# Identity products on TensorE ahead of five local stages, elements 0 and 1, in a two-layer sequence kernel

## What is computed

```python
xn = layernorm(x)
x = x + gated_linear_attention(xn) + local_transformer(xn)     # layer 0
xn = layernorm(x)
x = x + delta_rule_attention(xn) + switch_head_attention(xn)   # layer 1
```

```python
q, k, v = split(shift_token(x) @ wqkv)
q, k = rotary(l2norm(q) * qs), rotary(l2norm(k) * ks)
x = x + softmax(q @ k.T in the window) @ v @ wo
a, g = split(layernorm(shift_token(x)) @ w1 + b1)
x = x + (a * gelu(g)) @ w2 + b2
```

## Time and profile before

| | us |
|---|---|
| median of 3 runs | 1227.69 (1219.04 to 1230.57) |
| the profiled execution | 1230.62 |
| its span, first to last instruction | 1229.3 |
| mean granted TensorE clock in it | 0.98 of full speed |

### The profile page before, as it was taken

How to read it: one execution, slowest core, us unless ns; L and a number is a source line. 1 busy time by engine, 2 the same in 40 slices (tenths; PEclk the granted TensorE clock), 3 DMA queues, 4 the chain that set the end, 5 groups by cost and what they waited for, 6 DMA issues and landing times.

```text
span 1229.3 us, 30949 instructions
## 1 busy us (share of the span) xinstructions
PE 1153.7 (94%) x11842; PEld 918.7 (75%) x11842; DVE 906.9 (74%) x1894; ACT 704.4 (57%) x2020; POOL 837.9 (68%) x1156
## 2 busy tenths in 40 slices
PE   5887879999989999999999999999999999999998
PEld 3454558887768878777887887887778977788886
DVE  4947888986788868975587688987678766764544
ACT  5787787566756564466654666456776433332222
POOL 3745378688688745699579728699659837874870
PEclk9888889999999999999999999999999999999999
DMA  7101085765546575864478447785346867886763
GB/s 263 35 24 50 6 268 181 215 193 173 168 139 194 201 224 172 259 215 152 137 235 258 147 164 254 221 264 171 124 120 225 263 193 249 249 283 211 263 235 106
DMA packets 91186, 230.67 MB, mean 188 GB/s; under 512 B 9888, under 2 KB 16160, under 8 KB 90912
## 3 DMA queue, kind: packets, MB, share of 16 engines
q1 hardware_dynamic: 90896, 228.11, 57.8%
q10 hardware_dynamic: 144, 0.59, 0.1%
HBM read 225.51 MB, written 3.15 MB: 186 GB/s over the span
## 4 chain that ended last, share of the span: by engine, by line
PE 28%; DVE 12%; DMA 5%; POOL 4%; ACT 4%; issue 3%; SPq 1%; DVEq 0%; POOLq 0%; ACTq 0%
PE bank L896 8%; PE bank L943 6%; DVE ogate L1351 2%; PE bank L824 2%; POOL vgate L1737 2%; DMA kv<-values 2%; PE bank L933 2%; PE bank L914 2%; DMA vgate<-gates 2%; PE bank L610 1%; PE bank L924 1%; DVE kv L1120 1%; PE bank L907 1%; PE bank L669 1%; DMA gates<-xn 1%
## 5 line engine op out<-in xcount | busy, mean ns | idle before, releaser
L1737 POOL TENSOR_TENSOR vgate<-vgate,xT 128x512 f32<-128x512 f32 x256 | 324.9, 1293 | 68.7 <-DMA vgate<-gates 68.6
L896 PE MATMUL bank<-wv,vgate 128*128 128x128 f32 x2048 | 253.0, 278 | 0.6 <-POOL vgate L1737 0.4
L896 PEld LDWEIGHTS bank<-wv,vgate 128*128 128x128 f32 x2048 | 244.4, 193 | 9.6 <-issue 4.5
L943 PE MATMUL bank<-ogate,wo 128*128 128x256 f32 x1024 | 243.1, 383 | 1.7 <-DVE ogate L1351 1.4
L943 PEld LDWEIGHTS bank<-ogate,wo 128*128 128x128 f32 x1024 | 188.3, 190 | 31.8 <-issue 6.8
L1351 DVE TENSOR_TENSOR ogate<-ogate,bank 128x1024 f32<-128x1024 f32 x128 | 152.2, 1213 | 25.7 <-PE bank L933 19.1
L1621 ACT ACTIVATE mprob<-bank,mmin 128x256 f32<-128x256 f32 x128 | 59.3, 469 | 122.2 <-DVE mmin L1340 122.1
L1462 ACT ACTIVATE prob<-prob,mx 128x128 f32<-128x128 f32 (+1 forms) x256 | 96.0, 377 | 37.8 <-DVE mx L1056 37.4
L1669 POOL TENSOR_TENSOR rot<-rot 128x512 f32<-128x512 f32 x64 | 81.5, 1273 | 44.6 <-DVE rot L1032 44.5
L610 PE MATMUL bank<-wqkv,hT 128*128 128x512 f32 x192 | 107.0, 664 | 2.5 <-ACT hT L1398 1.4
L1714 POOL TENSOR_TENSOR dlt<-dlt,step 128x126 f32<-128x126 f32 (+22 forms) x248 | 92.8, 374 | 19.4
(11 more groups left out here) (224 smaller groups left out, 2354.2 us busy)
## 6 DMA issues: line engine op xcount, KB each, us to landing
ogate<-gates SPq DMA_DIRECT2D x128, 512.0 KB, 4.5
vgate<-gates SPq DMA_DIRECT2D x128, 512.0 KB, 4.4
wo<-in_wo_moe SPq DMA_DIRECT2D x128, 256.0 KB, 4.9
wv<-in_wv_moe SPq DMA_DIRECT2D x128, 256.0 KB, 4.8
kv<-values SPq DMA_DIRECT2D x64, 256.0 KB, 5.4
local<-in_local SPq DMA_DIRECT2D x1, 1715.0 KB, 9.5
wqkv<-in_wqkv SPq DMA_DIRECT2D x2, 768.0 KB, 6.4
x<-in_x SPq DMA_DIRECT2D x8, 128.0 KB, 5.0
```

What stands on the lines that cost most here:

```text
L896: i = nc.tensor.matmul(out[:, n * D:(n + 1) * D], xg[:, e, n * P:(n + 1) * P], m.wv[slot][:, e, :], start=(q, n, e) == (0, 0, 0), stop=(q, ...
L943: i = nc.tensor.matmul(out[:, 0:T], m.wo[slot][:, e, :], cg[:, e, :], start=(h, q, e) == (0, 0, 0), stop=(h, q, e) == (MH - 1, 1, EQ - 1))
L1737: i = tt(gate[:, e:e + half, :], gate[:, e:e + half, :], spread(m.xT[b % 2][:, :], 1, half), ALU.mult)
```

## The change

A helper `fill` issues one 128x128 product of the identity with itself into the first 128 columns of the bank that the stage has just taken. Five stages call it between the wait for the bank and the wait for the data, for elements 0 and 1 alone. The stage's own products then overwrite the result. No semaphore, bank or turn changes.

```diff
+    def fill(b, out):
+
+        if b < 2:
+            nc.tensor.matmul(out[:, 0:P], ident, ident, start=True, stop=True)
...
     def qkT(b, l, n, k):
         bank = banks.of("qkT", b, l, n, k)
         out = take(bank)
+        fill(b, out)
         pe.wait_ge(s.rot_scaled, nth("scale", b, l, n, k))
...
     def probT(b, l, w):
         out, p = take(bank), prob_of(m, b, l, w)
+        fill(b, out)
         pe.wait_ge(s.snorm, nth("score", b, l, w))
...
     def pv(b, l, w):
         out = take(bank)
+        fill(b, out)
         pe.wait_ge(t.emptied, t.use)
...
     def lnorm(b, l):
         out = take(bank)
+        fill(b, out)
         pe.wait_ge(s.h2shift, nth("hff", b, l))
...
     def hnT(b, l):
         take(bank)
+        fill(b, bank.ap)
         pe.wait_ge(h.emptied, h.use)
```

## The result

The changed kernel takes 1232.4 us, the median of 20 runs, against 1225.6 us for the kernel before, also the median of 20. The ratio is 1.0058, with a 95% interval of [1.0042, 1.0074]: 7.1 us slower by the ratio, 6.8 us by the two medians. That is within 1% and within the predicted range. But the forecast was "no change", and the interval excludes it. One execution of the changed kernel, 1653.9 us at a mean granted clock of 0.65, was in a slow state and is left out of the ratio; the other 19 lie between 1226.0 and 1240.8 us.

What follows compares the result with a forecast made beforehand. TensorE was taken to set the pace from about 176 us, after a chain passing between engines. 1230.6 + 3.0 - 3.2 = 1230.4 us against the profiled execution, 2.9 us above the median, gave 1227.5 us, no change; range 1216 to 1238.

Steps and rivals of the forecast that it cites:

- +3.0 - 3.2 = -0.2 us: Early part: uncovered fills in four unbroken TensorE runs cost 3.0 us; two clock falls gone or halved give back 3.2 us.
- the falls at 99.1 and 170.8 us: Early half-clock pieces: the one at 170.8 us gone, 1.6 us; the one at 99.1 us half gone, 1.6 us.
- The piece from 31 us: Half-clock piece after waits at 28 to 32 us: two fills, issued by 29.4 us, leave most of 3.29 us empty.
- 17 fills cost nothing: Early waits for data: 17 of 56 fills fall into 17 waits, nearly all longer than 0.24 us, which hide them.
- Removed: nothing. Moved: nothing, on any engine or queue: Whole kernel: the change only adds 56 fills, 13.7 us of TensorE work, and removes or moves nothing.
- Loss: Early part: 39 uncovered fills delay the stages, 10.8 us, to 1238.5 us, or 1241.8 us with another clock fall; chance 0.10.
- No effect on the clock: Early waits: two or three products are too little, the clock falls where it fell; 1230.7 us, chance 0.18.
- Gain: Early part: fills keep the clock up almost everywhere; 1218.7 us, or 1210.5 us if every cold us counts; chance 0.22.
- The last sentence of the prediction: If line 896's first product comes on time yet the end moves over 5 us, the dense part changed for an unnamed reason.

Runs made afterwards that it cites:

- the 17 alone: The changed kernel with products only at the 17 stages that had a wait ahead of them, the other 39 left out: 1230.4 us, ratio 1.0035 to before.
- elements 4 and 5: The change's 56 products issued for elements 4 and 5, whose local stages lie in the dense part, instead of 0 and 1: 1243.6 us, ratio 1.0133 to before.

## Why the prediction was wrong

**Cost and clock came out as a small balance.** The forecast was +3.0 - 3.2 = -0.2 us. The clean measurement is the change with 72 empty waits, +0.7 us give or take 2.5. That shows the balance, not its two terms: both may be small, or larger and equal. The mean granted clock did rise, to 0.985 in the 19 runs of the change and 0.987 in the 12 with the 72 waits, from 0.982 in the 88 runs of before on three chips and 0.980 with 184 empty waits. As forecast, the falls at 99.1 and 170.8 us went; one more, near 119 us, was not expected to. These pieces prove little by themselves, since the profile with 184 empty waits and no product lacks the last two as well. What is left at half clock before 180 us sums to some 31 us instead of 44.2. The piece from 31 us stayed although two fills stand ahead of it, as argued. The line "17 fills cost nothing" fits too: at 1.0035 the 17 alone lose as much as 61 instructions that do no work, at 1.0036, with the gap in the same burst.

**The step that failed** is the opening of the sum: "Removed: nothing. Moved: nothing, on any engine or queue", and with it "what it can delay is that stage and all of TensorE's work behind it until the next wait absorbs the delay". It counts instructions by their duration alone. They also have a place in a stream that is fetched in packets of 256, and 184 more of them move every border behind. The term left out measures 5.6 us, between 2.7 and 8.6, with 184 empty waits and no product. With the 0.7 us of the products and no shift it makes 6.3 us, for 7.1 measured, which the intervals do not tell apart. The profile carried the warning in a row that the prediction never used, q8 with its 95 packets.

**The rivals.** "Loss" foresaw a loss, by uncovered products that move the waits; it would have left the change with the 72 waits as slow as the change, and that one is level with before. Its 10.8 us were never approached, except in elements 4 and 5, where few waits are left and 17.1 us were lost. "No effect on the clock" is refuted by the mean clocks of the runs just given. "Gain" described a change that was not made: with the waits really full the clock up to 180 us is 0.97 to 0.99, and the gain is 3 to 5 us and not the 9 or 17 us of that case. The rule of the Trainium skill's "TensorE: Matmul & The Clock Gate", Terms, would give about 22 us for the same 44.2 us, an estimate from that rule; with nearly all of them warm the runs gained 3 to 5 us and decide against it here. That the rest lies where other engines set the pace is the likely reason and wasn't isolated.

**The last sentence of the prediction** did its work: the product came on time, the end moved by over 5 us in the medians, and that pointed into the dense part.

**Open.** What sets the 5 to 6.5 us. In the change no packet came through q8 between 1075.8 and 1093.5 us. That pause alone is not lateness, since TensorE took 17.6 us for the 256 instructions up to 1090.0 us; then it took 2.0 us for the next 256. The queue of the data was near full in that time:

```profile
q1 hardware_dynamic: 1828, 4.78, 84.3%
q14 instruction: 1, 0.01, 0.2%
```

and in the next 5.4 us two came at once:

```profile
q1 hardware_dynamic: 599, 1.56, 77.9%
q8 instruction: 2, 0.03, 2.4%
```

That the data transfers hold a packet up is likely but not shown. The kernel with the 94 products has two stretches in which TensorE took 256 instructions in about 4 us, the first without a gap at its end and the second with one of 1.1 us:

```profile
422.00:425.80 3.80, 3.80 (x138) 3.59 (x134) 1.38 (x4) 2.54 (x8) 0.00 (x0) 1.00 0.12 39
1092.10:1096.50 4.40, 4.40 (x145) 4.09 (x134) 2.31 (x6) 1.17 (x3) 4.32 (x4) 1.00 1.02 378
```

The DMA engines are busy for 0.12 of the first and all of the second. But at 4.1 us and a share of 0.98 the first profile of before has no gap either, and no run took the transfers away.

The link from the gap in single profiles to the medians is argued, from the sizes (about 4 us of gap for 5.6 us) and from the places, which follow the length of the stream. The single profiles don't bear it out by their times: the one with 184 empty waits has the gap and is the fastest of its twelve runs (1224.1 us), the one of the change with 72 waits has none and is the slowest of its twelve (1231.0 us). From the first product of line 896 or its like to the end, before takes 1053.0 us without the gap and the change 1050.1 us with it. What scatters the executions of one kernel by 5 us around their median is open too.

## What to carry to other kernels

Adding instructions to a dense engine changes more than the sum of their durations: when a small edit costs a few us that no stage explains, look for waits ended by "issue" in bursts of tiny instructions and at the packets of the instruction queue, and repeat the edit with empty instructions of the same number; then with the number rounded up to the next 256. Here products that keep TensorE's clock up gained something only when sized to the waits they fill, and then 3 to 5 us of 1226. With effects of half a per cent, never rank two kernels by one profiled execution of each.

## What the runs showed of the hardware that was not expected

- TensorE's instructions arrive in packets of 256 (95 packets, 1.56 MB, for 24,464; ten gaps in 14 profiles, all at the same place of a group of 256). Where TensorE took the 256 instructions between two borders in 2.0 to 4.4 us, with the DMA engines near full, it stood still behind the second for 1.0 to 4.2 us in ten of thirteen cases (the three without stand at 4.0 to 4.1 us, one of them in the first profile of before). Behind seven of the ten the granted clock was then at half for 3.4 us, in one of them for 6.8 us; behind the other three it stayed full.
- 61 instructions that wait for nothing, in stages that wait anyway, cost 4.4 us at the end of the kernel by the ratio, 184 cost 5.6 us, and 72 on top of the change took its loss away.
- With 94 products sized to the early waits the granted clock up to 180 us was 0.99, with 68 it was 0.97, for 0.88 before and 0.91 with 56 single ones; no semaphore or bank was changed.
